# Layer 0 of a four-layer fp32 kernel: row sums of squares from token-ordered sums, their scales through DRAM, x replaced by the transposed sum

## The reference, cut to what matters

```python
# layer 0
ms = mean(x * x, -1);  h = x * (scale * rsqrt(ms + 1e-6))
u = h @ up_w.T;        val, gate = split(u)
h = val * gelu(gate);  hq = act_quant(h);  wq = weight_quant(down_w)
x = hq @ wq.T + x
# layer 1
n = x * rsqrt(mean(x * x, -1) + 1e-6)
x = x + alpha1 * attention(gamma1 * n + beta1)
x = x + alpha2 * swiglu(gamma2 * rmsnorm(x) + beta2)
# layer 2: per-batch adapter;  layer 3: layer norm plus a conditional shift
```

## Time and profile before

| what | us |
|---|---|
| median of 3 runs (814.89 to 815.43) | 814.99 |
| the profiled execution's own time | 815.97 |
| its span, first to last instruction | 813.9 |
| of it layer 0, until the last up-projection | 233 |
| attention | to about 430 |

### The profile page before, as it was taken

One profiled execution on the slowest core, in us unless ns is written; L12 is line 12 of the kernel. 1 busy time (PEld: TensorE's weight loads), 2 busy tenths in 40 slices (PEclk: granted clock), 3 DMA queues, 4 the chain that ended last, 5 costly groups with the idle time before them and its releaser, 6 DMA issues.

```text
span 813.9 us, 19536 instructions
## 1 busy us (share of the span) xinstructions
PE 783.1 (96%) x6860; PEld 630.4 (77%) x6860; DVE 541.9 (67%) x933; ACT 375.8 (46%) x729; POOL 402.9 (50%) x451
## 2 busy tenths in 40 slices
PE   8999999999999899999999999999999999999984
PEld 6788888888888898998988766676767677787772
DVE  4777777777789898898895555555454545444664
ACT  4244444444658688888875324322223222322332
POOL 3655555555596988888883531313131313101565
PEclk9999999999999999999999999999999999999997
DMA  8843333333320100000003087767667676592442
GB/s 248 234 79 78 77 77 77 77 77 78 77 41 7 38 3 1 0 0 0 0 2 104 22 262 234 233 180 223 194 201 205 183 208 193 181 374 98 156 167 104
DMA packets 73731, 97.57 MB, mean 120 GB/s; under 512 B 38608, under 2 KB 48016, under 8 KB 73552
## 3 DMA queue, kind: packets, MB, share of 16 engines
q1 hardware_dynamic: 71088, 92.68, 39.3%
q10 hardware_dynamic: 2592, 4.20, 1.4%
HBM read 67.23 MB, written 21.23 MB: 109 GB/s over the span
## 4 chain that ended last, share of the span: by engine, by line
PE 65%; POOL 16%; issue 8%; DVE 3%; DMA 3%; ACT 3%; SPq 1%; POOLq 1%; ACTq 0%; DVEq 0%
PE bank L1081 21%; PE bank L395 20%; PE bank L1095 11%; PE bank L1115 4%; POOL p_sb L848 4%; PE bank L412 3%; POOL mlp_in L186 2%; DMA early<-in_cond_w 2%; POOL mlp_in L190 2%; POOL x_sb L857 1%; POOL mlp_in L192 1%; POOL x_sb L1665 1%; POOL sums L1659 1%; POOL sums L1654 1%; POOL att_in_lo L195 1%
## 5 line engine op out<-in xcount | busy, mean ns | idle before, releaser
L1447 DVE TENSOR_TENSOR g<-bank,silu 128x512 f32<-128x512 f32 x64 | 44.2, 691 | 106.4 <-ACT silu L1292 56.6
L1292 ACT ACTIVATE silu<-bank 128x512 f32<-128x512 f32 x64 | 38.3, 598 | 111.3 <-PE bank L1081 111.3
L1298 ACT ACTIVATE g_hi<-g 128x512 fp32r<-128x512 f32 x64 | 40.4, 632 | 98.4 <-DVE g L1447 96.4
L395 PE MATMUL bank<-up_hi,xs_hi 128*128 128x512 f32 x256 | 83.0, 405 | 1.6 <-DVE h L620 0.8
L1450 DVE TENSOR_TENSOR g_lo<-g,g_hi 128x512 fp32r<-128x512 f32 x64 | 52.7, 824 | 45.3 <-ACT g_hi L1298 45.3
L395 PE MATMUL bank<-up_lo,xs_hi 128*128 128x512 f32 x256 | 80.6, 397 | 0.7 <-DVE up_lo L657 0.7
L1081 PE MATMUL bank<-mlp_in_hi,w_hi 128*128 128x512 f32 x256 | 80.6, 396 | 0.0
L848 POOL TENSOR_TENSOR p_sb<-p_sb,rec 128x512 f32<-128x512 f32 x64 | 66.7, 1046 | 27.6 <-DVE rec L1399 27.6
L1081 PE MATMUL bank<-mlp_in_lo,w_hi 128*128 128x512 f32 x256 | 79.8, 393 | 0.0
L1081 PE MATMUL bank<-mlp_in_hi,w_lo 128*128 128x512 f32 x256 | 79.7, 392 | 0.0
L395 PE MATMUL bank<-up_hi,xs_lo 128*128 128x512 f32 x256 | 79.4, 392 | 0.0
(11 more groups left out here) (193 smaller groups left out, 1916.3 us busy)
## 6 DMA issues: line engine op xcount, KB each, us to landing
gen_hyper<-in_gen_t SPq DMA_DIRECT2D x32, 512.0 KB, 4.9
gen_made<-base_w SPq DMA_DIRECT2D x64, 256.0 KB, 3.9
adapter_w<-gen_made SPq DMA_DIRECT2D x64, 256.0 KB, 3.5
tokens<-in_x_tok SPq DMA_DIRECT2D x32, 128.0 KB, 2.3
w_stage<-in_w_t SPq DMA_DIRECT2D x32, 128.0 KB, 2.4
weight_slot<-adapter_w SPq DMA_DIRECT2D x4, 1024.0 KB, 9.0
w_hi<-adapter_w SPq DMA_DIRECT2D x4, 1024.0 KB, 5.7
w_lo<-adapter_w SPq DMA_DIRECT2D x4, 1024.0 KB, 9.4
```

What stands on the lines that cost most here:

```text
L395: last = nc.tensor.matmul(bank[2 * j + part][:, :], (xs_hi, xs_lo)[a][:, k, d, :], up[b][:, d, at:at + 512], start=n == d == 0, stop=n == ...
L1292: nc.scalar.activation(silu[:, f % 2, :], bank[2 * (f % 2)][:, :], ACT.Silu).then_inc(S["silu_done"], 1)
L1298: nc.scalar.activation(gs[0][:, f % 2, :], g[:, f % 2, :], ACT.Copy).then_inc(S["g_hi_done"], 1)
L1447: nc.vector.tensor_tensor(g[:, f % 2, :], bank[2 * (f % 2) + 1][:, :], silu[:, f % 2, :], ALU.mult).then_inc(S["g_done"], 1)
```

## The change

- The old y, its transposes and the order of PE stay, but `y` now is the sum: DVE's `add_tokens` computes `y_ps * scale + tokens` in token order (lag 3), in place of `take_y` on ACT and `add_y` on DVE. For that the tokens are loaded a second time by SP into `tokens_again`, two buffers (`load_again`, lag 4).
- ACT's `take_x` copies the transposed sum from PSUM over x (lag 4).
- ACT's `square_rows` squares `y` with an accumulator, one number per token. `square`, `sum_squares`, `row_squares`, `take_row_squares`, `early_rstd` and `attention_rstd` are gone, and so is an unused bf16 identity.
- Every four tiles POOL's `row_scales` makes 128x4 scales with a power, SP stores them to DRAM in token order (`store_rows`) and loads them back, broadcast to all 128 partitions, into `stat` (`spread_rows`). `attention_input` waits for that load.
- SP's loop ends after eight extra steps, and waits for the last x (`x_done`) before layer 2's first loads.

```diff
@@ sync_program @@
         def transpose_q(s):
             if s.live(3):
                 k = s.slot(3, 2)
                 sp.wait_ge(Z["q_done"], s.at(3) + 1)
+                hold(sp, Z["sp_passed"])
                 wait(sp, Z["y_ready"], s.at(5) + 1 if s.live(5) else 0)
                 hold(sp, Z["sp_passed"])
                 sp.dma_start_transpose(qt[:, k], q[:, k]).then_inc(qt_loaded[k], 16)
+
+        def load_again(s):
+            if s.live(4):
+                k = s.slot(4, 2)
+                wait(sp, Z["y_done"], s.at(5) if s.live(5) else 0)
+                hold(sp, Z["sp_passed"])
+                sp.dma_start(again[:, k, :], io["x_tok"][:, bass.ds(s.at(4) * D, D)]).then_inc(again_loaded[k], 16)
+
+        def store_rows(s):
+
+            if s.slot(0, 4) == 2 and s.live(10):
+                sp.wait_ge(Z["row_rstd_done"], s.turn(10, 4))
+                hold(sp, Z["sp_passed"])
+                sp.dma_start(rstd_row[bass.ds(s.at(10) * P, 4 * P)].rearrange("(t p) -> p t", p=P),
+                             row_rstd[:, bass.ds(s.at(10), 4)], allow_slow_non_contiguous=True).then_inc(Z["row_stored"], 16)
+
+        def spread_rows(s):
+            if s.slot(0, 4) == 3 and s.live(11):
+                sp.wait_ge(Z["row_stored"], 16 * s.turn(11, 4))
...
+                sp.dma_start(stat[:, bass.ds(s.at(11) * P, 4 * P)],
+                             rstd_row[bass.ds(s.at(11) * P, 4 * P)].unsqueeze(0).to_broadcast([P, 4 * P])).then_inc(stat_loaded, 16)

         def body(s):

             transpose_q(s)
             wait(sp, Z["w1_lo_done"], s.at(3))
             load_stage(s)
             sp.wait_ge(Z["squared_done"], s.at(3))
             load_tokens(s)
+            load_again(s)
+            store_rows(s)
+            spread_rows(s)
@@ scalar_program @@
-    def take_y(act, s):
-        if s.live(3):
...
-            nc.scalar.activation(y[:], y_ps, ACT.Copy, scale=small[:, s.slot(3, 4), 3:4]).then_inc(Z["y_done"], 1)
+    def square_rows(act, s):
+
+        if s.live(3):
+            t = s.at(3)
+            act.wait_ge(Z["y_done"], t + 1)
+            wait(act, Z["rows_done"], t)
+            hold(act, Z["passed"])
+            nc.scalar.activation(squared_rows[:], y[:], ACT.Square, scale=D ** -0.5,
+                                 accum_out=row_squares[:, bass.ds(t, 1)]).then_inc(Z["rows_done"], 1)
+
+    def take_x(act, s):
         if s.live(4):
+            act.wait_ge(Z["yt_ready"], s.at(4) + 1)
             hold(act, Z["passed"])
+            nc.scalar.activation(x[:, :, bass.ds(s.at(4) * P, P)], yt_ps, ACT.Copy).then_inc(Z["x_done"], 1)
@@ scalar body @@
-            take_y(act, s)
+            take_x(act, s)
             gate(s, 0)
-            square(act, s)
+            square_rows(act, s)
...
             gate(s, 1)
-            if s.last(-3):
-                early_rstd()
@@ vector @@
-    def add_y(ve, s):
-        if s.live(4):
-            ve.wait_ge(Z["yt_ready"], s.at(4) + 1)
-            xt = x[:, :, bass.ds(s.at(4) * P, P)]
-            nc.vector.tensor_tensor(xt, xt, yt_ps, ALU.add).then_inc(Z["x_done"], 1)
+    def add_tokens(ve, s):
+
+        if s.live(3):
+            t, k = s.at(3), s.slot(3, 2)
+            ve.wait_ge(Z["y_ready"], t + 1)
+            ve.wait_ge(Z["y_scale_done"], t + 1)
+            ve.wait_ge(again_loaded[k], 16 * s.turn(3, 2))
+            wait(ve, Z["yt_ready"], t)
+            wait(ve, Z["rows_done"], t)
+            nc.vector.scalar_tensor_tensor(out=y[:], in0=y_ps, scalar=small[:, s.slot(3, 4), 3:4], in1=again[:, k, :],
+                                           op0=ALU.mult, op1=ALU.add).then_inc(Z["y_done"], 1)
```

POOL's new function, and the vector engine's order where attention starts:

```diff
+    def row_scales(pool, s):
+
+        if s.slot(0, 4) == 3 and s.live(7):
+            group = bass.ds(s.at(7), 4)
+            pool.wait_ge(Z["rows_done"], s.at(7) + 4)
...
+            nc.gpsimd.tensor_tensor(row_rstd[:, group], row_squares[:, group], wscale[:, 5:6].to_broadcast([P, 4]),
+                                    ALU.pow).then_inc(Z["row_rstd_done"], 1)
@@ vector, handover @@
-            first["add_y"](ve, e32)
+            first["add_tokens"](ve, e32)
             ve.wait_ge(A["v_cleared"], 1)
             take_values(a2)
-            first["take_row_squares"](ve, e32)
-            first["add_y"](ve, e33)
+            first["add_tokens"](ve, e33)
             maxima(a2, 0)
             maxima(a2, 1)
-            first["take_row_squares"](ve, e33)
-            first["add_y"](ve, e34)
             sums(a2, 0)
             sums(a2, 1)
+            first["add_tokens"](ve, e34)
             maxima(a2, 2)
```

More of the change, by code:

```diff
@@ L161, with attention_input @@
 V_OUTB, V_BD, V_BU, V_LNW, V_LNB, V_LINB, V_EVEN, V_ODD = 0, 2, 3, 5, 7, 9, 11, 12
-def attention_rstd(nc, act, core, t):
-    S = core["att_sems"]
-    st = core["stat"][:, bass.ds(t * GT1, GT1)]
-    nc.scalar.activation(st, st, ACT.Ln, scale=1.0 / D, bias=core["wscale"][:, 3:4]).then_inc(S["ln_done"], 1)
-    act.wait_ge(S["ln_done"], t + 1)
-    hold(act, S["passed"])
-    nc.scalar.activation(st, st, ACT.Exp, scale=-0.5).then_inc(S["rstd_done"], 1)
-def attention_input(nc, pool, core, t, k, part):
+def attention_input(nc, pool, core, s, part):
     x, cond, stat, h, S = core["x"], core["cond"], core["stat"], core["att_in"], core["att_sems"]
-    hi, lo = (parts[k] for parts in core["att_parts"])
+    t = s.at(0)
+    hi, lo = (parts[s.slot(0, 2)] for parts in core["att_parts"])
     hb = h[:].rearrange("p h (b l) -> p h b l", b=GB1)
@@ L271, in transpose_q @@
                 sp.dma_start_transpose(qt[:, k], q[:, k]).then_inc(qt_loaded[k], 16)
+        def load_again(s):
[13 more added lines that the diff above has]
+                sp.wait_ge(Z["row_stored"], 16 * s.turn(11, 4))
+                hold(sp, Z["sp_passed"])
+                wait(sp, stat_loaded, 16 * s.turn(11, 4) - 16)
+                hold(sp, Z["sp_passed"])
+                sp.dma_start(stat[:, bass.ds(s.at(11) * P, 4 * P)],
+                             rstd_row[bass.ds(s.at(11) * P, 4 * P)].unsqueeze(0).to_broadcast([P, 4 * P])).then_inc(stat_loaded, 16)
         def body(s):
@@ L306, in sync_program @@
                 transpose_q(Step(3, 3, N))
-        pipeline(sp, N, 0, 4, body, start=4)
-        for t in range(N, N + 3):
-            transpose_q(Step(t, t % 4, N))
+        pipeline(sp, N, 11, 4, body, start=4, stop=N)
+        for t in range(N, N + 8):
+            s = Step(t, t % 4, N)
+            transpose_q(s)
+            load_again(s)
+            store_rows(s)
+            spread_rows(s)
     def split_tile(pool, s):
@@ L413, in down @@
             last.then_inc(Z["y_ready"], 1)
-    def row_squares(pe, s):
-        if s.live(5):
-            pe.wait_ge(Z["sq_sum_done"], s.at(5) + 1)
-            wait(pe, Z["ss_done"], s.at(5))
-            pe.wait_ge(Z["x_done"], s.at(3) if s.live(3) else N)
-            nc.tensor.matmul(ss_ps, core["ones"][:], sq_sum[:, s.slot(5, 2), :], start=True, stop=True).then_inc(Z["ss_ready"], 1)
     def y_transposes(pe, s):
@@ L427, in y_transposes @@
             wait(pe, Z["x_done"], s.at(3))
-            if not s.live(5):
-                wait(pe, Z["ss_done"], s.at(5))
             for d in range(DH):
@@ L467, in tensor_program @@
         warm(WARM // 2)
-        pipeline(pe, N, 5, 4, body, stop=N)
+        pipeline(pe, N, 4, 4, body, stop=N)
     def square_tokens(act, s, lag):
@@ L634, in body @@
         def body(s):
-            add_y(ve, s)
+            add_tokens(ve, s)
             quantise(ve, s)
@@ L658, in vector_program @@
                                     up[0][:, :, at:at + 512].bitcast(FP32), ALU.subtract).then_inc(Z["up_lo_done"], 1)
-        pipeline(ve, N, 5, 4, body, stop=N)
+        pipeline(ve, N, 4, 4, body, stop=N)
     return dict(sems=Z, sync=sync_program, gpsimd=gpsimd_program, tensor=tensor_program, scalar=scalar_program, vector=vector_program,
-                w1_low=w1_low, sum_squares=sum_squares, down=down, row_squares=row_squares, y_transposes=y_transposes,
-                square=square, take_y=take_y, add_y=add_y, quantise=quantise,
-                y_scale=y_scale, take_row_squares=take_row_squares)
+                w1_low=w1_low, row_scales=row_scales, down=down, y_transposes=y_transposes,
+                square_rows=square_rows, take_x=take_x, add_tokens=add_tokens, quantise=quantise, y_scale=y_scale)
 def mlp_input(nc, pool, core, t, k, parts):
@@ L762, in layers @@
         Z, N0 = first["sems"], T // P
-        e32, e33, e34, e35, e36 = (Step(t, t % 4, N0) for t in range(N0, N0 + 5))
+        e32, e33, e34, e35 = (Step(t, t % 4, N0) for t in range(N0, N0 + 4))
         a1, a2 = (Step(t, t % 2, NA) for t in (1, 2))
@@ L1130, in _ @@
             values(a2)
-            first["row_squares"](pe, e32)
             first["y_transposes"](pe, e32)
@@ L1135, in _ @@
             keys(a2)
-            first["row_squares"](pe, e33)
             first["y_transposes"](pe, e33)
@@ L1278, in attention_body @@
                 if s.first_tile(3):
```

(11 more changed lines are left out.)

118 lines of the change are left out of this document (38 added, 80 removed).

## The result

| | before | changed |
|---|---|---|
| median, us | 815.21 (4 runs, 814.89 to 816.79) | 871.82 (4 runs, 866.3 to 873.57) |
| ratio to before | | 1.068 (95% interval 1.063 to 1.073) |
| span of the profiled execution, us | 813.9 | 864.5 |
| mean granted clock | 0.992 | 0.967 |
| DMA packets | 73,731 | 83,715 |

The change makes the kernel 56.6 us slower. The forecast was 9.6 us slower, and its range ended at 832.

A forecast was written before the change was run, and what follows sets the result against it. PE, busy 96% of the span, was taken to bound the kernel, with a 7.12 us loop replacing it in layer 0. Terms 10.8 - 0.2 - 1.0 = +9.6 gave 824.6 us from the median 814.99; range 814 to 832.

The forecast's parts named there:

- The loop of one turn: Layer 0, q to q through the second token load and add_tokens: 7.12 us a turn against PE's 6.59.
- Where it starts: Layer 0, body 3: the first second token load lets DVE start add_tokens at 41.3 us.
- two irregular turns: Layer 0: tokens 1.6 us late and a transpose issue 0.9 longer, both added to the loop, 233.5 to 236.0.
- The last up-projection: End of layer 0 on PE: ends at 244.1 us instead of 233.3, so +10.8.
- The handover and attention: After layer 0: handover -0.2 us in sum, attention -1.0 from ACT operations no longer needed.
- the DRAM round trip of the scales: Eight stores of 512 four-byte numbers and eight broadcasts: cost 0, or up to 1 us each, 8 in all.
- SP's idle 4.0 us a turn: Layer 0: SP's idle time, 3.5 us with the second token load, said to cover the round trip's issues.
- Rival 3: Round trip: stores hold the queue or extra traffic lengthens landings, another microsecond a group, 833 us; chance 0.13.
- Rival 4: Layer 0: PE's stalls of 0.5 us a tile bring its clock down, 835 us or more; chance 0.03.

The follow-up runs named there:

- e1: Changed kernel without the stores and broadcast loads of the scales, stat filled with ones instead: 831.81 us, ratio 1.021.
- e3: Changed kernel with the second token load one step earlier and no DRAM round trip of scales, stat filled with ones: 810.51 us, ratio 0.996.
- e9: Changed kernel with the stores of the first six groups issued from ScalarE's queue, at lag 8 in place of 10: 876.01 us, ratio 1.073.
- e2: Changed kernel with the second token load one step earlier (lag 3 in place of 4), round trip kept: 840.81 us, ratio 1.032.
- e4: Kernel before the change plus the eight stores, of ones that nobody reads, not waited for until layer 0 is over: 823.00 us, ratio 1.010.
- e11: Changed kernel with each broadcast load of scales four steps later (lag 15 in place of 11), stores unchanged: 860.11 us, ratio 1.054.
- e10: Changed kernel with the same 512 pieces of 4 bytes a store, each written 64 bytes behind the last: 833.10 us, ratio 1.019.
- e8: Changed kernel with the earlier second load, scales turned into rows on TensorE, stores of four 512-byte rows, last store and spread later: 812.51 us, ratio 0.998.
- e5: Changed kernel with each store written as 128 pieces of 16 bytes in place of 512 of 4: 833.64 us, ratio 1.023.
- e7: Changed kernel without the round trip of groups 0 to 5, only the last two groups stored and spread: 839.26 us, ratio 1.030.

## Why the prediction was wrong

- **The loop of one turn was right.** 7.12 us was the sum; the changed kernel shows 7.03 in the undisturbed turn above, e1 7.16 over 27 turns. PE alone could do 6.6, as e3 shows. Link by link the first turn above has 0.16 us from q to the transpose (0.14 in the sum, of which 0.02 for a semaphore was in no row), 0.64 from tokens to the new load (0.57), 2.36 to add_tokens (2.52), 0.40 to h (0.37) and 0.79 to q (0.86).
- **Where it starts was 3 us too late.** Add_tokens of body 3 was put at 41.3 and ran at 37.94 in e1: SP issued the transpose of that step at 33.15 there, and at 36.37 in before, from which the row was taken. Why it came sooner I don't know. The 27 turns took 1.3 less than the sum with its two irregular turns, and from the last add_tokens to PE it was 0.7 more. The last up-projection ended at 240.2, +6.9 and not +10.8.
- **The handover and attention were 4.9 us too low**: forecast -1.2, and by e1 +3.7 (10.6 less 6.9). In e1's windows PE's clock dips to 0.66 behind the gaps that the late add_tokens leave, which the sum had at the full clock:

```profile
255.00:260.00 5.00, 4.17 (x60) 3.65 (x52) 2.57 (x6) 1.57 (x5) 2.05 (x2) 1.00 0.01 3
260.00:265.00 5.00, 3.29 (x18) 3.10 (x22) 3.02 (x8) 3.35 (x9) 2.45 (x4) 0.66 0.00 0
```

  The two errors cancel: +10.6 at the mark without the round trip, +9.6 forecast.
- **The step that failed is the DRAM round trip of the scales**, "so I take 0; if a store also held up the next turn, its cost would be up to 1 us each, 8 in all". It cost 40 us (871.82 less 831.81), 5 a group in the mean. Two things in it were wrong. Its landing was bounded by the nearest rows, 2.3 and 3.1 us, but none of those writes to DRAM at all, and it took 10. And only the store's own landing and a hold of up to 1 us were costed, not what a slow store does to other transfers: the second loads beside the slow stores took 4.0 to 8.2 us instead of 2.3, in a loop that had just lost its slack (e9, and e2 to e4). SP's idle 4.0 us a turn, named as the cover, did cover SP's own issues and, in layer 0, its wait for the landing (see e11); it covers nothing of the held loads.
- **Rival 3** had the right mechanism in its second half ("the extra traffic makes landings longer"), at a fifth of its size and with a chance of 0.13. Its first half, that the stores hold the queue, is not it (e9), and its sign, a wait before the transpose of q, did not come: behind the store at 111.35 the transpose is issued 0.16 us after q ends, at 114.97. What came were late loads. The rule cited with it (the Trainium skill, DMA: Bandwidth & Descriptors, Rules for kernel authors: one descriptor per element) agrees with the trace: in e9, where ACT's queue carries this store alone, it shows 528 packets for it. But by e10 their number is not what costs: as many pieces land in 2.2 us when they start 64 bytes apart.
- **Rival 4** was right that the clock can fall, but not from stalls of 0.5 us a tile: in e1, whose turns have only those, it was 1.00 from 100 to 200 us, with PE busy for 96.4 of 100. In the changed kernel it was 0.95 there, with PE busy for 87.8: it fell behind the stores' long turns, where PE had stood still for microseconds (0.66 in 125 to 130, above), and again at the handover.
- **Behind the mark** another 2 to 8 us come up in the profiled executions of all variants. Of e1's 16.8 us of longer span 10.6 stand at the mark, 1.2 more by 742 us of its span (where before is at 730), and 5.0 after that, where in e1 PE has a gap and a lower clock that before's trace doesn't have. The same part of the program in before, and then in e1:

```profile
778.00:784.00 6.00, 5.88 (x136) 4.90 (x135) 3.93 (x7) 2.46 (x4) 3.86 (x4) 1.00 0.61 229
784.00:790.00 6.00, 5.21 (x104) 4.24 (x104) 3.92 (x7) 2.46 (x4) 3.86 (x5) 1.00 0.25 90
```

```profile
790.00:796.00 6.00, 2.94 (x27) 2.37 (x22) 2.31 (x4) 0.09 (x1) 4.16 (x4) 0.83 0.57 208
796.00:802.00 6.00, 6.00 (x135) 5.09 (x134) 3.69 (x6) 2.36 (x4) 2.20 (x2) 0.89 0.25 90
```

  e3 has the gap too, in the execution that was profiled (span 812.6); others of e3 had spans near 807. I found no cause for it; it stays open, and so does why the 6.5 us of e3 and 6.7 of e8 at the mark are only 3.3 and 1.6 in the medians.

**Also open:** at the last store of the changed kernel DVE stood still for 6.2 us and ACT for 4.7 with no releaser that the trace names, and PE's matmuls came one at a time, until the store had landed. Two fetches of instructions by DMA fall into that stretch, so they may have been held as the loads were. That was not tried by itself. e2, e9 and e11, which have the same last store, show such a standstill too (6.3, 4.0 and 5.3 us on DVE), and e1, e5 and e10, without a slow store, show none; but e7, with the same last store, shows none either.

## What to carry to other kernels

A transfer has two prices, its own landing and what it does to every other transfer under way; a small one can be the dearer of the two, and idle DMA engines don't vouch for it. So turn a vector that lies across partitions into rows before it is written, or at least don't write it to DRAM as single numbers side by side: pieces of 16 bytes, or the same numbers 64 bytes apart, took away nearly all of the price here. And when a load's step stands behind the result that its own reader releases, count the loop from issue to issue: the sum of its links was within 0.1 us of the measured turn here, and issuing the load one step earlier removed the loop.

## What the runs showed of the hardware that was not expected

- Stores of 512 numbers of 4 bytes, side by side in DRAM, landed in 9.7 to 10.6 us where SP stood waiting for them; the same 512, each 64 bytes from the next, in 2.2 (e10); the same bytes in pieces of 16 in 1.7 (e5). The packets of the slow store at 111.35 had gone out within about 1.5 us of the issue.
- While such a store is in flight, transfers of another queue wait as well, the SBUF-to-SBUF transpose among them: 9.3 us instead of 3.1, and loads of 128 KB 7.8 to 8.1 us instead of 2.3 (e9).
- In the changed kernel PE's granted clock fell from 1.00 to 0.56 and 0.50 over windows of 5 us in which PE was busy 1.63 and then 0.69, and it stood at 0.50 from 305 on, through a window in which PE was busy for all of its 5 us.
